# Image tokens of the second layer: operands turned over, four context chunks in four column tiles, in two steps

## The reference, cut to what matters

```python
ip_ehs = encoder_hidden_states[:, -NUM_TOKENS:]        # 8 batches x 4 tokens x 512
k_ip = heads(ip_ehs @ W_k_ip)                          # 32 tokens x 320
v_ip = heads(ip_ehs @ W_v_ip)                          # 32 tokens x 320
ip_n = _l2norm(ip_ehs)                                 # needs one norm per token
sem = jnp.einsum('bhse,bne->bhsn', qsem, ip_n)
fused = attn_scores + SEM_SCALE * sem
ip_out = jnp.einsum('bhsn,bhnd->bhsd', probs_ip * spatial_mask[None, None, :, None], v_ip)
```

## Time and profile before

| | us |
|---|---|
| median of 3 runs | 816.89 (816.88 to 821.27) |
| profiled execution, its own time | 819.18 |
| its span in the trace | 817.4 |
| TensorE busy | 782.5 (96%) |
| VectorE busy | 560.0 (69%) |
| ScalarE busy | 425.0 (52%) |
| mean granted TensorE clock | 0.981 |

### The profile page before, as it was taken

One profiled execution on the slowest core, in us unless ns is written; L12 is line 12 of the kernel. 1 busy time (PEld: TensorE's weight loads), 2 busy tenths in 40 slices (PEclk: granted clock), 3 DMA queues, 4 the chain that ended last, 5 costly groups with the idle time before them and its releaser, 6 DMA issues.

```text
span 817.4 us, 17243 instructions
## 1 busy us (share of the span) xinstructions
PE 782.5 (96%) x6392; PEld 635.2 (78%) x6392; DVE 560.0 (69%) x1531; ACT 425.0 (52%) x911; POOL 402.6 (49%) x297
## 2 busy tenths in 40 slices
PE   5989899999999999999999999999999999988896
PEld 5877787888888878787877778787887888766574
DVE  5357345757575857677858778788697797687744
ACT  5234523655546474646465465565555655555551
POOL 6421202201102040403658976887779768779763
PEclk9999989999999999999999999999999999999998
DMA  8975631847546564546443345245062342500010
GB/s 266 219 210 151 178 111 54 227 135 190 128 146 162 179 153 132 158 118 159 114 112 121 94 108 167 64 113 156 35 184 86 86 116 66 139 1 16 21 34 16
DMA packets 103027, 100.67 MB, mean 123 GB/s; under 512 B 10264, under 2 KB 102176, under 8 KB 102944
## 3 DMA queue, kind: packets, MB, share of 16 engines
q1 hardware_dynamic: 101408, 98.26, 43.5%
q10 hardware_dynamic: 1536, 1.31, 0.5%
HBM read 61.65 MB, written 36.74 MB: 120 GB/s over the span
## 4 chain that ended last, share of the span: by engine, by line
PE 76%; DVE 7%; issue 4%; DMA 4%; POOL 4%; ACT 3%; SPq 2%; POOLq 0%; DVEq 0%; ACTq 0%
PE pB L379 22%; PE pB L495 13%; PE pB L458 8%; PE pB L481 7%; PE pB L579 5%; PE pPV L522 4%; PE pPV L517 4%; PE pPV L527 4%; PE pB L536 3%; POOL Y L1278 3%; PE pPV L513 2%; DMA KP<-k0d 2%; DVE m_sb L1041 2%; DVE m_sb L1043 1%; ACT P L842 1%
## 5 line engine op out<-in xcount | busy, mean ns | idle before, releaser
L1278 POOL TENSOR_TENSOR Y<-P,wv 128x512 f32<-128x512 f32 x120 | 156.5, 1321 | 106.8 <-ACT P L842 106.6
L1058 DVE TENSOR_TENSOR Y<-pB,Y 128x512 f32<-128x512 f32 x160 | 108.8, 686 | 70.5 <-PE pB L495 60.6
L458 PE MATMUL pB<-KP,QP 96*128 96x256 f32 x640 | 129.8, 288 | 4.4 <-DMA KP<-k0d 3.2
L458 PEld LDWEIGHTS pB<-KP,QP 96*128 96x128 f32 x640 | 106.6, 191 | 18.4 <-issue 7.4
L1255 POOL TENSOR_TENSOR klo<-xin,khi 128x256 fp32r<-128x256 f32 x18 | 13.3, 758 | 216.8 <-ACT khi L753 216.8
L1043 DVE TENSOR_REDUCE m_sb<-pB 128x2 f32<-128x504 f32 x160 | 108.0, 675 | 11.2 <-PE pB L458 9.5
L481 PE MATMUL pB<-QP,KP 100*128 100x512 f32 x320 | 109.2, 421 | 2.4 <-DMA QP<-mlo 2.0
L842 ACT ACTIVATE P<-pB 128x512 f32<-128x512 f32 x160 | 86.5, 596 | 43.7 <-PE pB L481 33.8
L842 ACT ACTIVATE P<-pB,ln 128x512 f32<-128x512 f32 x160 | 101.3, 692 | 0.0
L832 ACT ACTIVATE wv<-pB 128x512 fp32r<-128x512 f32 x120 | 66.8, 591 | 56.6 <-PE pB L481 55.3
L753 ACT ACTIVATE Vs<-pPV 128x512 f32<-128x512 f32 (+1 forms) x80 | 39.4, 493 | 101.5 <-PE pPV L517 68.2
(11 more groups left out here) (175 smaller groups left out, 1718.2 us busy)
## 6 DMA issues: line engine op xcount, KB each, us to landing
QP<-q0d SPq DMA_DIRECT2D x64, 192.0 KB, 4.1
KP<-k0d SPq DMA_DIRECT2D x64, 192.0 KB, 4.4
c_sb<-in_cT SPq DMA_DIRECT2D x16, 512.0 KB, 5.2
q0d<-qhi SPq DMA_DIRECT2D x32, 256.0 KB, 2.5
k0d<-khi SPq DMA_DIRECT2D x30, 256.0 KB, 2.5
q0d<-qlo SPq DMA_DIRECT2D x16, 256.0 KB, 2.8
k0d<-klo SPq DMA_DIRECT2D x15, 256.0 KB, 2.8
VB<-vipd SPq DMA_DIRECT2D x6, 640.0 KB, 3.9
```

The lines of the kernel that those rows point to most:

```text
L458: made = mm(bank[:, sc * S:sc * S + S], QP[i][0:KROWS, j, a, sc * 128:sc * 128 + 128], KP[i][0:KROWS, j, :], start=True, stop=True)
L1058: tt(Y[:, p, dst, :], bank_of["gp", q, dst][:, :], Y[:, p, dst, :], MUL).then_inc(dv_y, 1)
L1278: tt(Y[:, p, ch, :], P[:, p, ch, :], PH[q % HR][ch].bitcast(F32), SUB).then_inc(po_y, 1)
```

## The change

The entry of the plan is split: part 0 stays at the end of step 3 of unit 1, part 1 comes at the end of step 5. In part 0 each of the four context chunks of `cip` (128x32) is a weight in a column tile of its own, and the matching chunk of `wki1` (then `wvi1`) moves with 320 columns. The four partial sums land under each other in one bank, at partitions 0, 32, 64 and 96. ScalarE copies them to SBUF (`parts`, over the chunk 0 of `wki1` and `wvi1`, which is read by then). The norms take one matmul with 128 columns, and VectorE adds the four chunks. In part 1 the partial sums are added by matmuls against `stack`, four 32x32 identities under each other: `parts` as weights and `stack` moving gives the transposed keys and values, `stack` as weights and `parts` moving gives the values with tokens on partitions. VectorE makes `stack` and the squares earlier, in step 9 of unit 0 (`image_sums`).

```diff
+IP_AT = ((1, 3), (1, 5))
...
-    if (u, j) == (1, 3):
-        out += [("ip",)]
+    if (u, j) in IP_AT:
+        out += [("ip", IP_AT.index((u, j)))]
...
+        Y_flat = Y[:, :, :, :].rearrange("p a b c -> p (a b c)")
+        stack = t1_all[:, 0:B * NIP]
+        parts = [Y_flat[:, EC * C * i:EC * C * i + C] for i in range(2)]
...
@@ tensor_program
-                    pe.wait_ge(*((ac_ip, 1), (dv_ip, 1), (dv_ip, 2), (ac_ip, 3))[a])
+                    pe.wait_ge(*((ac_ip, 1), (ac_ip, 2), (dv_ip, 1), (ac_ip, 3), (dv_ip, 2), (ac_ip, 5))[a])
...
-                    for m in range(KC):
-                        M = CHUNK[m]
                         for k in range(EC):
-                            made = mm(bank[0:M, 32 * m:32 * m + 32], w[:, k, m * 128:m * 128 + M], cip[:, k, :],
-                                      start=(k == 0), stop=(k == EC - 1))
+                            made = mm(bank[32 * k:32 * k + 32, 0:C], cip[:, k, :], w[:, k, :], start=True, stop=True,
+                                      tile_position=(0, 32 * k))
...
-                for k in range(EC):
-                    made = mm(bank[:, 0:32], ones[:, :], csq[:, k, :], start=(k == 0), stop=(k == EC - 1))
+                    mm(bank[:, 0:128], ones[:, :], cs[:, 128:256], start=True, stop=True).then_inc(pe_ip, 1)
...
-                for k in range(EC):
-                    made = mm(bank[0:B * NIP, 0:C], cip[:, k, :], wvi1[:, k, :], start=(k == 0), stop=(k == EC - 1))
+                    pe.wait_ge(dv_set, 4)
+                    for i in range(2):
+                        bank = take("ip", 3 + i)
+                        pe.wait_ge(ac_ip, i + 1)
+                        for m in range(KC):
+                            M = CHUNK[m]
+                            made = mm(bank[0:M, 32 * m:32 * m + 32], parts[i][:, m * 128:m * 128 + M], stack, start=True, stop=True)
+                        made.then_inc(pe_ip, 1)
+                        give(bank)
+                    bank = take("ip", 5)
+                    mm(bank[0:B * NIP, 0:C], stack, parts[1], start=True, stop=True).then_inc(pe_ip, 1)
...
@@ scalar_program
+                if part == 0:
+                    for i in range(2):
+                        ac.wait_ge(pe_ip, i + 1)
+                        copy(parts[i], bank_of["ip", i][:, 0:C]).then_inc(ac_ip, 1)
...
@@ vector_program
+            def image_sums():
+                dv.wait_ge(l_w["const"], 16 * 6)
+                dv.wait_ge(l_w["ident"], 16)
                 tt(csq[:, :, :], cip[:, :, :], cip[:, :, :], MUL).then_inc(dv_set, 1)
+                nc.vector.tensor_reduce(stack, ident[:, :].rearrange("p (k n) -> p n k", n=B * NIP), AX, ADD).then_inc(dv_set, 1)
+
+            def image_tokens(part):
+                if part == 0:
+                    dv.wait_ge(pe_ip, 3)
+                    then(nc.vector.tensor_reduce(nrm[:, :], bank_of["ip", 2][:, 0:128].rearrange("p (k n) -> p n k", n=B * NIP), AX, ADD))
+                    settled()
+                    nc.vector.tensor_scalar(nrm[:, :], nrm[:, :], 1e-24, None, ALU.max).then_inc(dv_ip, 1)
+                else:
+                    dv.wait_ge(ac_ip, 4)
...
+                    if (u, j) == (0, 9):
+                        image_sums()
...
@@ sync_program
-                        sp.wait_ge(pe_ip, 4)
+                        sp.wait_ge(pe_ip, 6)
```

More of the change, by code:

```diff
@@ new lines, in image_tokens @@
+            def image_tokens(part):
+                if part == 0:
+                    for i, w in enumerate((wki1, wvi1)):
+                        bank = take("ip", i)
+                        pe.wait_ge(l_w["ip1"], 32)
+                        pe.wait_ge(l_w["const"], 16 * 6)
+                        for k in range(EC):
+                            made = mm(bank[32 * k:32 * k + 32, 0:C], cip[:, k, :], w[:, k, :], start=True, stop=True,
+                                      tile_position=(0, 32 * k))
+                        made.then_inc(pe_ip, 1)
+                        give(bank)
+                    bank = take("ip", 2)
+                    pe.wait_ge(dv_set, 3)
+                    mm(bank[:, 0:128], ones[:, :], cs[:, 128:256], start=True, stop=True).then_inc(pe_ip, 1)
+                    give(bank)
+                else:
[6 more added lines that the diff above has]
+                            made = mm(bank[0:M, 32 * m:32 * m + 32], parts[i][:, m * 128:m * 128 + M], stack, start=True, stop=True)
+                        made.then_inc(pe_ip, 1)
+                        give(bank)
+                    bank = take("ip", 5)
+                    mm(bank[0:B * NIP, 0:C], stack, parts[1], start=True, stop=True).then_inc(pe_ip, 1)
+                    give(bank)
@@ L673, in tensor_program @@
                         elif what == "ip":
-                            image_tokens()
+                            image_tokens(*a)
                 for _ in ahead:
@@ L862, in image_weights, with image_tokens @@
                 act(ex[:, :, :, :], t1[:, :, :, :], ACT.Exp, scale=0.25).then_inc(ac_ex, 1)
[L864 to L873, removed]
+            def image_tokens(part):
+                if part == 0:
+                    for i in range(2):
+                        ac.wait_ge(pe_ip, i + 1)
+                        copy(parts[i], bank_of["ip", i][:, 0:C]).then_inc(ac_ip, 1)
+                else:
+                    ac.wait_ge(pe_ip, 4)
+                    bank = bank_of["ip", 3]
+                    copy(kip[:, 0:2, :], bank[:, 0:64].rearrange("p (c n) -> p c n", n=32))
+                    copy(kip[0:64, 2, :], bank[0:64, 64:96]).then_inc(ac_ip, 1)
+                    ac.wait_ge(pe_ip, 5)
+                    bank = bank_of["ip", 4]
+                    copy(vhi[:, 0:2, :], bank[:, 0:64].rearrange("p (c n) -> p c n", n=32))
+                    copy(vhi[0:64, 2, :], bank[0:64, 64:96]).then_inc(ac_ip, 1)
+                    ac.wait_ge(pe_ip, 6)
+                    copy(vip, bank_of["ip", 5][0:B * NIP, 0:C]).then_inc(ac_ip, 1)
             def image_weights_back(u):
@@ L1151, in last_output, with image_tokens @@
                                                    ADD, ADD).then_inc(dv_op, 1)
-            def image_tokens():
+            def image_sums():
                 dv.wait_ge(l_w["const"], 16 * 6)
+                dv.wait_ge(l_w["ident"], 16)
                 tt(csq[:, :, :], cip[:, :, :], cip[:, :, :], MUL).then_inc(dv_set, 1)
[L1156 to L1161, removed]
+                nc.vector.tensor_reduce(stack, ident[:, :].rearrange("p (k n) -> p n k", n=B * NIP), AX, ADD).then_inc(dv_set, 1)
+            def image_tokens(part):
+                if part == 0:
+                    dv.wait_ge(pe_ip, 3)
+                    then(nc.vector.tensor_reduce(nrm[:, :], bank_of["ip", 2][:, 0:128].rearrange("p (k n) -> p n k", n=B * NIP), AX, ADD))
+                    settled()
+                    nc.vector.tensor_scalar(nrm[:, :], nrm[:, :], 1e-24, None, ALU.max).then_inc(dv_ip, 1)
+                else:
+                    dv.wait_ge(ac_ip, 4)
+                    bank = bank_of["ip", 4]
+                    low(vlo[:, 0:2, :], bank[:, 0:64].rearrange("p (c n) -> p c n", n=32), vhi[:, 0:2, :])
+                    low(vlo[0:64, 2, :], bank[0:64, 64:96], vhi[0:64, 2, :]).then_inc(dv_ip, 1)
             def image_values(u):
                 b = u % B
-                dv.wait_ge(dv_ip, 1)
+                dv.wait_ge(dv_ip, 2)
                 dv.wait_ge(l_hm, 16)
@@ L1326, in gpsimd_program @@
                             image_step(*a)
-                        elif what == "ip":
-                            po.wait_ge(dv_ip, 2)
+                        elif what == "ip" and a[0] == 0:
+                            po.wait_ge(dv_ip, 1)
                             tt(invip[:, :], nrm[:, :], mhalf[:, 0:B * NIP], POW).then_inc(po_ip, 1)
```

26 lines of the change are left out of this document (7 added, 19 removed).

## The result

| | before | changed |
|---|---|---|
| median of 6 runs each, us | 817.53 (816.88 to 821.27) | 812.33 (809.63 to 814.08) |
| ratio | | 0.9921, 95% interval 0.9900 to 0.9942 |
| profiled execution, its own time | 819.18 | 809.63 |
| its span | 817.4 | 807.8 |

The kernel became faster, by 0.8%, where 1.2% was forecast. The time, 812.33, lies 4.9 us above the forecast and 0.3 us above the range's end. I had drawn the line between "faster" and "same" at one per cent and given 0.71 to the first and 0.27 to the second; this comparison falls in the second. The two profiled executions differ by 9.55 us, as forecast (9.45), but the timed medians by 5.2 only. The experiments are about this gap.

A forecast was written before the change was run, and what follows sets the result against it. TensorE, busy 782.5 of 817.4 us, was taken to bound the kernel. Removing 13.00 us and adding 1.61 and 1.94 leaves 9.45 us off the median of 816.89, so 807.4 us, with a range of 804.5 to 812.0.

The forecast's parts named there:

- What bounds the kernel: Whole span: TensorE, busy 782.5 of 817.4 us, bounds it; what leaves its stream leaves the span unless a wait replaces it.
- Step one: Part 0, end of step 3 of unit 1: two tiled rounds, in and out, and norms take 1.61 us of TensorE.
- step two: Part 1, end of step 5 of unit 1: six small matmuls, one long one and a mode change take 1.94 us.
- The rival of tiles one after the other: Column tiles do not overlap: 810.7 us, or 809.2 if only weight loads run in a row; chance 0.07 for both.
- The waits: Around both new parts in unit 1: TensorE gets no new wait, and VectorE and ScalarE are ready in time.
- The rival that VectorE is late: At the second part VectorE comes late and the clock falls behind it: 2.6 us lost, 810.0 us; chance 0.08.
- The clock: TensorE's granted clock stays at 1.00 from 108 to 140 us, where the old block had fallen to about 0.50.
- the rival's 0.13: The clock falls anyway, in the second part or between the parts: 1.7 us lost, 809.1 us; chance 0.13.
- what is removed: 13.00 us: Old image-token block in unit 1: 12.48 us of TensorE plus 0.52 us on the scores and maximum behind it.
- slower than before: Later units shift in time and the clock falls behind six more gaps: 10.2 us lost, 817.6 us; chance 0.03.

The follow-up runs named there:

- e2: Kernel before with its 32 old matmuls unchanged but spread over four places of unit 1; ratio 0.9970 against the kernel before.
- e3: Changed kernel without column tiles, the four chunks as weights one after the other, adding up in one bank; ratio 0.9965 against the kernel before.
- e7: Changed kernel with the six matmuls of 32 moving columns in its second part made four times over; ratio 1.0007 against the kernel before.
- e8: Changed kernel with the last matmul of its second part, 320 moving columns, made nine times instead of once; ratio 0.9975 against the kernel before.
- e4: Changed kernel with its second part right behind the first, at the end of step 3 of unit 1; ratio 0.9909 against the kernel before.
- e10: Changed kernel with tile t1 declared at its old place, so no tile has moved against the kernel before; ratio 0.9877 against the kernel before.
- e12: Kernel before, run once more with no edit, for another trace; ratio 1.0003 against the kernel before.
- e9: Kernel before with tile t1 declared where the change declares it, so later tiles lie at the changed kernel's addresses; ratio 0.9987 against the kernel before.

## Why the prediction was right in its mechanism and 2 us off in size

**What bounds the kernel: right.** TensorE's time left the span with nothing in its place; in the two first traces, whose starts (111.59 and 111.50) and ends (76.5 and 75.9) happen to be alike, the transposes of the maxima come 9.3 us earlier for units 2 to 7 and 9.0 for the later ones.

**Step one, forecast 1.61, measured 1.46; step two, forecast 1.94, measured 2.14.** Together 3.60 for 3.55, the nearness of the sum being luck. In step two a price was too low: of the 32 records in the first 3.01 us two are the end of the maximum ahead of them, so a weight of 128 columns costs 3.01 / 13 = 0.23 us and not 0.215, and e2's twelve such matmuls in 2.38 us say 0.24. That is 0.12 of the 0.20. Four tiles cost little more than one matmul: 1.22 us for the eight in tiles, 0.61 a round, and 4.43 without (e3), 0.55 each. The rival of tiles one after the other falls, in both forms. The Trainium skill, "TensorE: Matmul & The Clock Gate", part 3, says that a weight load overlaps a running matmul only where the row group differs; by that step one would have taken 3.4 us. The trace disagrees, as `weigh` had.

**The waits: right.** VectorE waited 0.47 us for the norms. Its second wait, for ScalarE's copy of the values, I had put at nothing; it was 0.44 us, and hid. The bank that waits for `dv_op` cost nothing. The rival that VectorE is late did not occur.

**The clock: right in direction.** It stayed at 1.00 in unit 1 in every trace of the unaltered change. That sparse matmuls were the cause was argued then; e7 and e8 show it, in one trace each. The 1.5 us of sparse matmuls that the change leaves did not trip it in three traces, nor in e4 and e10. But e2's 2.4 us in one piece did so once of twice, and so did e3's second step, 1.6 us of them on 32 rows. So there is no safe margin here, and the rival's 0.13 was not too much.

**What failed is the term of the sum "what is removed: 13.00 us".** I read the price of the old block off one execution and took it off the median of all. It is right for that execution: between the two first traces the blocks differ by 9.21 us (27.06 - 17.85) and the spans by 9.6. But e12 and e9 show the old block at 24.0, a removal of 9.8 us, hence a gain of 6.1. Three comparisons of the unaltered change gave ratios of 0.9921, 0.9909 and 0.9879, that is 6.5, 7.5 and 9.9 us; their intervals overlap. By means over all their runs, 18 of the changed kernel at 812.2 and 51 of before at 819.8, it is 7.6 us, with an interval of 6.5 to 8.8. That lies between the two values and fits neither alone, if nothing outside the block differs. That the executions of before are a mix of the two I infer from this; in what shares, five traces don't measure.

**The rest of the first comparison's shortfall is spread.** Its six runs of before had a median of 817.53, where 23, 29 and 22 later ones, on three chips, had 820.20, 819.53 and 821.00. Executions of either kernel differ by 5 us or more for reasons outside the block: the start takes 110.2 to 116.3 us, the end 74.5 to 78.6, and the ends of the changed kernel reach from 75.9 to 78.5. I asked whether the change lengthens start or end, since the first traces of before had the shortest. Addresses do not (e9, e10), and e12 has a start of 114.58, longer than two of the three of the unaltered change, and an end of 78.55, longer than all three. A small effect on either cannot be excluded by so few traces.

The end goes with the place of one late fall of the clock. In the six traces whose end takes 74.5 to 76.5 us, it comes 19 to 21 us ahead of the last mark; in the six with 78.3 to 78.6, within 0.3 us of that mark; in e7 and e8, with 77.1 and 77.9, 18 us ahead. The first two groups hold both kernels. The kernel before in its first trace (mark at 740.9), then in e12 (mark at 741.3), columns as above:

```profile
722.50:725.50 3.00, 3.00 (x10) 0.50 0.02 5
741.60:744.90 3.30, 2.43 (x15) 1.00 0.02 6
```

```profile
722.50:725.50 3.00, 3.00 (x16) 1.00 0.02 5
741.60:744.90 3.30, 3.30 (x10) 0.50 0.02 6
```

That the fall makes the end longer is argued from this; no run moved it. What makes SP issue the row of the maxima at another time in each execution stays open.

**The rival "slower than before"** asked for six more falls of the clock in the later units. There are two or three near the end in every trace, before and after alike. It did not come.

A version better than the changed kernel did not appear: e4 and e10 are the same within their intervals.

## What to carry to other kernels

A price read off one trace holds for an execution, and a stretch in which TensorE's clock falls has no single price: take several traces of the old kernel before subtracting it, and cut the spans at marks to see what is constant. In this kernel matmuls with 32 moving columns cost twice: by their weight loads, 0.24 us for a weight of 128 columns where one with ten times the moving columns took 0.55, and by the clock that they let fall for the work behind them. So let the small operand be the weight, in column tiles, and let the long one move. Spreading such work out did less than turning it over (2.5 us against 7.6), and splitting the turned work into steps did nothing (e4).

## What the runs showed of the hardware

- TensorE's clock fell from 2.4 to 1.2 GHz while TensorE was busy without a gap, with 32 moving columns in each matmul (before, 1.00 and then 0.50; e7, 1.00 and then 0.50), and not with 320 (e8, 1.00 over 4.96 us; e3, 1.00 over 4.43 us). Pieces of 1.6 us (e3) and 2.4 us (e2) were followed by a fall once each, and one of 2.4 us (e2) was not.
- The moment differs between executions of one program, 2.6 to 5.7 us into the same block, and with it the block's time by 3.1 us (27.06 and 23.95).
- Four column tiles with weights of 32 columns and 320 moving fp32 columns each take little more than the time of one: 1.22 us for two rounds, 4.43 for the eight in a row.
- Executions of one program differed by 4.8 us in the start (changed kernel, 111.5 to 116.3), with TensorE's wait for one 20 KB transfer between 2.3 and 5.7 us.
